# Where the first projection of the next batch stands among the score units of an attention body

## The reference

```
xn = layernorm(x)                               # x: [16, 512, 128]
q, k, v = xn @ Wq, xn @ Wk, xn @ Wv             # 16 heads of width 8
q, k = q / |q|, k / |k|
attn = softmax(causal(8 * q k^T))               # [512, 512] for each head and batch
out = x + (attn @ v) @ Wo + experts(xn)         # top 2 of 8 experts, each 128 -> 512 -> 128
```

## Time and profile before

| what | value |
|---|---|
| median of 3 runs | 671.65 us (671.43 to 672.34) |
| the profiled execution's own time | 673.31 us |
| its span, first to last instruction | 671.5 us |
| around the span (673.31 - 671.5) | 1.8 us |
| attention, bodies 0 to 7 | about 89 to 253 us of the span |
| experts | about 254 to 508 us |
| attention, bodies 8 to 15, and the last output | about 508 to 671 us |
| one body in the middle of a stage | 19.0 to 19.4 us |
| granted TensorE clock, mean of the span | 0.976 |

### The profile page before, as it was taken

One profiled execution on the slowest core, in us unless ns is written; L12 is line 12 of the kernel. 1 busy time (PEld: TensorE's weight loads), 2 busy tenths in 40 slices (PEclk: granted clock), 3 DMA queues, 4 the chain that ended last, 5 costly groups with the idle time before them and its releaser, 6 DMA issues.

```text
span 671.5 us, 21426 instructions
## 1 busy us (share of the span) xinstructions
PE 617.3 (92%) x7417; PEld 413.1 (62%) x7417; DVE 462.8 (69%) x1296; ACT 450.5 (67%) x689; POOL 417.7 (62%) x585
## 2 busy tenths in 40 slices
PE   2977468999999999999999999999999999999985
PEld 2756322434444447999999999999995444444343
DVE  7699986666667875454544446778665688888856
ACT  3999546888888885444444444444448888888893
POOL 6356627777777877775700016777654777777783
PEclk9999858999999999999999999999999999999998
DMA  6997685464455558945432234445443456654541
GB/s 174 274 289 243 186 253 108 100 116 103 99 132 125 126 109 174 245 131 143 132 80 73 70 82 115 108 122 121 111 102 78 92 128 126 141 112 110 131 107 48
DMA packets 186592, 89.36 MB, mean 133 GB/s; under 512 B 115456, under 2 KB 176032, under 8 KB 186400
## 3 DMA queue, kind: packets, MB, share of 16 engines
q1 hardware_dynamic: 178192, 70.70, 44.3%
q0 software_dynamic: 8336, 17.84, 9.2%
HBM read 30.17 MB, written 32.24 MB: 93 GB/s over the span
## 4 chain that ended last, share of the span: by engine, by line
PE 78%; DVE 5%; ACT 4%; issue 3%; DMA 1%; POOL 1%; DVEq 0%; ACTq 0%; POOLq 0%; SPq 0%
PE psum L1075 19%; PE psum L1063 18%; PE psum L955 16%; PE psum L923 8%; PE psum L883 7%; PE psum L907 2%; PE psum L944 2%; ACT prob L813 2%; PE psum L966 2%; PE psum L914 2%; ACT prob L766 1%; DMA qks<-dup 1%; DVE dup L1236 1%; PE psum L846 1%; POOL prob L666 1%
## 5 line engine op out<-in xcount | busy, mean ns | idle before, releaser
L813 ACT ACTIVATE prob<-psum 128x1536 f32<-128x1536 f32 x192 | 267.1, 1454 | 56.5 <-PE psum L923 54.8
L823 ACT ACTIVATE prob<-psum,prob 128x256 f32<-128x256 f32 x284 | 117.3, 470 | 132.4 <-PE psum L1063 131.4
L650 POOL DMA_INDIRECT rows<-slot_y,idx x128 | 131.2, 1025 | 46.0 <-issue 27.6
L652 POOL DMA_INDIRECT slot_x<-rows,slots x128 | 127.6, 997 | 36.1 <-issue 31.2
L955 PE MATMUL psum<-prob,v 128*18 128x448 f32 (+3 forms) x2048 | 136.4, 385 | 5.0 <-POOL prob L666 5.0
L1075 PEld LDWEIGHTS psum<-prob 128*128 128x128 f32 x1136 | 137.8, 192 | 3.6
L666 POOL TENSOR_SCALAR_AFFINE_SELECT prob<-prob 128x384 f32<-128x384 f32 (+2 forms) x224 | 104.3, 475 | 56.3 <-ACT prob L813 54.5
L1075 PE MATMUL psum<-prob 128*128 128x128 f32 x1136 | 138.1, 275 | 0.0
L1063 PE MATMUL psum<-xs,prob 128*128 128x256 f32 x568 | 134.9, 381 | 0.5 <-DVE xs L1464 0.4
L1063 PEld LDWEIGHTS psum<-xs,prob 128*128 128x128 f32 x568 | 102.6, 191 | 12.4 <-issue 0.9
L955 PEld LDWEIGHTS psum<-prob,v 128*18 128x18 f32 x2048 | 48.5, 98 | 92.6 <-issue 73.0
(11 more groups left out here) (159 smaller groups left out, 664.4 us busy)
## 6 DMA issues: line engine op xcount, KB each, us to landing
slot_y<-xs SPq DMA_DIRECT2D x71, 128.0 KB
xs<-in_L_attn_x SPq DMA_DIRECT2D x16, 256.0 KB, 4.3
prob<-in_L_ffn_W SPq DMA_DIRECT2D x16, 256.0 KB, 3.6
xn_rows<-prob SPq DMA_DIRECT2D x16, 256.0 KB, 2.9
xn_cols<-xts SPq DMA_DIRECT2D x16, 256.0 KB, 3.1
xt<-xn_cols SPq DMA_DIRECT2D x16, 256.0 KB
rows<-xn_rows SPq DMA_DIRECT2D x16, 256.0 KB, 3.5
out<-acc SPq DMA_DIRECT2D x15, 256.0 KB
```

Of the source, the lines that this page charges most:

```text
L650: pool.indirect_dma_start(rows[:, j, c, t, :], None, done, where).then_inc(moved[j], 16)
L652: pool.indirect_dma_start(slot_x, where, halves_of_rows[:, j, 0, t, :], None).then_inc(moved[j], 16)
L813: act.activation(prob[:, KEPT[k], :], score[k % 2], ACT.Exp, scale=SCALE / UP ** 2)\
L823: act.activation(hs[:, s, c, :], psum[:, 2 * s + c // 2, (c % 2) * FT:(c % 2 + 1) * FT], ACT.Gelu, bias=ws[:, s, B1C + c:B1C + c + 1]).the ...
```

## The change

In bodies 1 to 14 the call of `project(b + 1, 0)` moves one unit forward: it stands behind unit 0, and no longer behind unit 1. Nothing is added or taken away, and no wait is changed.

```
                 for k in range(UN):
                     scores(b, par, k)
-                    if k == 1 and not last and not known(b, 0):
+                    if k == 0 and not last and not known(b, 0):
                         project(b + 1, 0)
                     elif k == 2 and not fresh:
                         weigh(b - 1, 1 - par, 8)
```

## The result

The changed kernel takes 675.81 us (median of 14 runs, 673.24 to 677.53); the kernel before, run beside it, 672.16 us (14 runs, 671.21 to 676.58). The ratio on record (it isn't the quotient of the medians) is 1.0049, with a 95% interval of 1.0036 to 1.0061: slower by about half a per cent. The forecast was 674.8 us in a range of 672.1 to 677.3. The profiled execution took 676.94 us with a span of 675.2, against 673.31 and 671.5 before.

The account below looks back on a forecast made before the run. The prediction took TensorE, busy 92% of the span, as the bound, movable only through its waits. It added 0.14 (first stage), 0.80 (body 8) and 2.22 us (bodies 9 to 14), 3.16 us, to 671.65: 674.8 us, range 672.1 to 677.3.

Parts of the forecast that it names:

- What bounds the kernel: Whole kernel: TensorE, busy 92% of the span, is the bound; its work is unchanged, so only its waits can move the time.
- The projection's own work: Between units 0 and 1: work moved, not added; unit 1 ends 0.84 us later, everything from unit 2 on starts as before.
- Unit 1's exponential: On ScalarE in ordinary bodies: it starts 0.72 us later, not 0.84, since it was held 0.12 us until now.
- The new wait: Ahead of unit 3: TensorE stands still 0.37 us for the exponential of unit 1; bodies 9 to 14 pay 2.22 us.
- The signs that the forecast named: In the changed kernel's profile: idle times and waits, such as 0.3 to 0.4 us ahead of unit 3, that would show it right.
- the step on the first stage: Bodies 1 to 7: the wait ahead of chunk 0 takes up the delay, leaving 0.02 us a body, 0.14 us in all.
- rival C: Ahead of chunk 0, bodies 1 to 7: earlier `evacuate` and unit 3 not held remove 2.0 us; 669.65 us, chance 0.08.
- Body 8: Unit 3 there already waits for the exponential of unit 1, so the whole delay is paid: 0.80 us.
- Rival A: At the projection's new place: late loads of `xt` add 1.24 us each; 676.05 us with one; chance 0.24.
- Rival B: Ordinary bodies: unit 3 doesn't wait, unit 1 reaching ScalarE under 0.47 us later; no change, 672.1 us, chance 0.14.

## Why the prediction came out as it did

**What bounds the kernel** held in part: TensorE's instructions were the same, and waits decided in the second stage. "Only its waits can move the time" did not hold: the same instructions up to chunk 8 take TensorE 0.39 us less in an ordinary body (217.16 - 213.92 = 3.24; before 218.18 - 214.55 = 3.63).

**The projection's own work** was mis-sized. I took 0.84 us, from its start to unit 2. Ahead of unit 1 it takes 215.90 - 215.15 = 0.75. In body 10 the end piece of unit 1 starts at 549.38 - 546.50 = 2.88 us into the body, where it was 547.78 - 545.63 = 2.15: 0.73 later.

**Unit 1's exponential** came later, but by 0.53 us and not by 0.72: in body 6 it starts 217.22 - 213.92 = 3.30 us into the body, in body 10 549.80 - 546.50 = 3.30 too, where it was 548.40 - 545.63 = 2.77. Of the missing 0.19, 0.11 is the projection; the rest is the handover from the start of the end piece to ScalarE, 217.22 - 216.80 = 0.42 us, where unit 0's, from which I took it, is 0.50 in both kernels.

**The new wait** is there in every body, as the step said. Unit 3 starts 4.81 us into the body in place of 4.62 (218.73 - 213.92; 219.17 - 214.55): 0.19 later where I had 0.37. That follows: 0.53 less the slack of 0.35 that the forecast had read. The idle time is longer than that, 0.51 us, since TensorE arrives sooner; this part of it costs nothing. Bodies 9 to 14 pay 0.19 each, 1.14 us and not 2.22. The signs that the forecast named came in kind, with other sizes: 0.51 us of idle time ahead of unit 3 (0.3 to 0.4 forecast), 0.44 ahead of unit 1's exponential (0.7), 4.9 us of such waits in the second stage (4.2), 1.53 in body 8 (1.3), 1.77 ahead of the copy into `v` (2.1), and no wait ahead of chunk 0.

**What the step on the first stage missed.** "Everything from unit 2 on would start as before" and "chunk 8 stays where it is" are the sentences that failed. TensorE gets through unit 1 and unit 2 faster: 0.28 us where the pieces of line 923 are neighbours (0.36 for 0.32 + 0.32), and 0.09 on the projection. The trace of before held a sign of it. In its body 6 twelve matmuls of line 923 stand in a row and take 228.74 - 228.20 = 0.54 us to the next row, not twice the 0.32 of six:

```profile
228.20 0.61 PE L923 MATMUL psum<-qks 32*128 32x448 f16 x12
228.74 1.06 PE L955 MATMUL psum<-prob,v 128*18 128x320 f32 x16
```

So chunk 8 and the copy into `v` come 0.38 us sooner (218.29 - 213.92 = 4.37, before 219.30 - 214.55 = 4.75), line 1242 takes 0.22 us and not 0.56, and `evacuate` starts 0.43 us sooner, now held by chunk 9 alone. The wait ahead of chunk 0, which is 0.34 us from start to start, goes altogether, against unit 3's 0.19: a body is 0.16 us shorter, where I had it 0.02 longer. That is the place of rival C, with its copy of line 1242; it came in although unit 3 was held, which I had called its condition. By body 8 this had gained the 0.73 us of the profile, with some 0.2 us lost to a late load of `xt`.

**Body 8** was right in kind: most of the delay is paid. Unit 3 comes 0.62 us later (512.34 - 507.55 = 4.79, before 512.45 - 508.28 = 4.17), and the body costs 0.5 us where the clock stays (18.85 and 18.88 us), less than the 0.80 of the forecast. It costs 1.4 us where the clock falls behind the 1.53 us of idle time (19.76 and 19.79).

**What it had no term for.** Body 12 waits for GpSimd's masks 1.42 us in place of 0.86, 1.4 us or more in every profile with bodies 9 to 14 moved, where it is 0.86 to 0.97 in those without. The lines of before and of the change:

```profile
593.91 1.06 PE L955 MATMUL psum<-prob,v 128*18 128x448 f32 x16 [0.86 <-POOL prob L666]
597.17 1.06 PE L955 MATMUL psum<-prob,v 128*18 128x448 f32 x16 [1.42 <-POOL prob L666]
```

The body is 0.63 us longer, 0.44 beyond the 0.19 of an ordinary one. Body 10 ends in a wait for the transposes of 1.70 us where it was 0.43.

**Rival A** was true in the profiles, in bodies 3 and 5 (0.15 to 0.7 us). It isn't what the time shows: without those waits it was the same. The estimate of 2.6 us for this load, from the Trainium skill, "DMA: Bandwidth & Descriptors", section "Anatomy of one DMA", is from a fit to transfers that GpSimd issues; this load is issued by SyncE, and no run shows its landing. **Rival B**'s condition, less than 0.47 us of delay for unit 1 on its way to ScalarE, wasn't met: it was 0.73 - 0.08 = 0.65.

So the direction was right, and so was the mechanism in the second stage and in body 8. The first stage went the other way, and the total came out partly by luck: 0.9 + 1.1 us less cost than forecast in the bodies of the first and the second stage, and 0.6 + 0.4 + 1.3 us more in bodies 8, 12 and 10.

**What stays open.** Why the transposes at the end of body 10 are late. TensorE waits there for 0.93 to 2.50 us in all eleven profiles of kernels with an edit in bodies 1 to 8 (in the one with chunk 9 ahead and the projection at the old place the wait, 0.93 us, is put down to ScalarE). It waits for 0 to 0.43 us in the three profiles in which bodies 1 to 8 are those of before. So the lateness goes with what was changed ahead of body 10, also where body 10 itself is unchanged, and the change seems to carry it; by what way isn't shown, and the pattern rests on one or two profiles a kernel. By the bodies that are understood, the change costs about 1 us (-1.1 + 1.1 + 0.5 + 0.4); the late transposes add 1.3 and the fallen clock 0.9 in the profiles that have them. How often either comes in a run can't be read from one profile a kernel.

## What to carry to other kernels

Moving work ahead of a producer delays its consumer: compare the delay with the slack that the buffer's reuse has, and then follow the chain of exponentials, since a covered wait comes back at the next unit with little ahead of it. When a group of instructions is taken out from between two others, read from the trace what those two cost as neighbours; a sum of single durations doesn't tell it. The loss can be turned: with chunk 8 between units 1 and 2, chunk 9 ahead of unit 3 and body 8 left at the old place, half a per cent of loss became a small gain. Its bodies fit that: 0.1 us in the second stage is about what the projection's new place saves (0.75 for 0.84), and the 0.46 in the first stage (18.90 for 19.36) is about that and the lost wait ahead of chunk 0.

## What the runs showed of the hardware

The 32-row matmuls of line 923 take little longer in larger groups: two take 0.32 us to the next row, six 0.32, eight 0.36, twelve 0.54. The Trainium skill, "TensorE: Matmul & The Clock Gate", section "Part 3: Packing small matmuls — row/col tiling", has small matmuls on different groups of rows of the array run at once. The trace fits that: the rows of line 923 work on 32 partitions each, and six such matmuls take no longer than two. That this is why two units side by side are cheaper is argued from the durations, not shown by an experiment on the groups of rows. It may not be the whole reason, since two chunks of line 955, on 128 partitions, take 1.85 us as neighbours and 0.99 each apart.

The granted clock fell from 1.00 to 0.50 (2.4 to 1.2 GHz) in body 8 in two of four profiles with the same 1.53 us wait of unit 3, and stayed at 1.00 in the other two. Where it fell, it cost 0.9 us (19.76 and 19.79 us for 18.85 and 18.88). Behind the late transposes it is the same: of ten profiles with a wait of 1.43 to 2.50 us at the end of body 10, three show the clock at 0.50 in body 11 (waits of 1.43, 1.52 and 2.50 us), which is 1.0 to 1.5 us longer there than body 9, and seven show 1.00 (waits of 1.45 to 1.89 us). In this kernel such a wait is a risk and not a fixed price.
